# Head attention of a two-stage network: v loaded densely a batch at a time and spread by GpSimd; the TensorE loop moved within its 256-instruction blocks

## What is computed

```python
q, k, v = xs @ Wq.T, xs @ Wk.T, 2 * (xs @ Wv.T)        # 25088 positions, 8 heads x 16
q, k, v_h = _l2norm(q), _l2norm(k), _l2norm(v)
attn_head = softmax(einsum('bnhd,bngd->bnhg', v_h, v_h))      # 8 x 8 a position
q = einsum('bnhg,bngd->bnhd', attn_head, q)
k = einsum('bnhg,bngd->bnhd', attn_head, k)
attn = softmax(einsum('bnhd,bnhe->bnde', k, q))               # 16 x 16 a position
out = einsum('bnhd,bnde->bnhe', v, attn)
out = transpose(out, (0, 3, 1, 2)).reshape(b, n, 128) @ proj_w.T + proj_b
```

## Time and profile before

| what | us |
|---|---|
| three runs | 3550.62, 3564.91 (median), 3569.99 |
| the profiled execution, its own time | 3554.55 |
| its span in the trace | 3552.8 |
| the attention stage in it, about | 1990 to 3424 |
| TensorE's loop in it (33 times) | 2071 to 3313.7 |
| TensorE busy, share of the span | 3015.3 (85%) |
| TensorE weight loads busy | 2232.1 (63%) |
| VectorE busy | 1937.6 (55%) |
| ScalarE busy | 1269.4 (36%) |
| GpSimd busy | 567.8 (16%) |

### The profile page before, as it was taken

One profiled execution on the slowest core, in us unless ns is written; L12 is line 12 of the kernel. 1 busy time (PEld: TensorE's weight loads), 2 busy tenths in 40 slices (PEclk: granted clock), 3 DMA queues, 4 the chain that ended last, 5 costly groups with the idle time before them and its releaser, 6 DMA issues. The chain is left out here.

```text
span 3552.8 us, 145120 instructions
## 1 busy us (share of the span) xinstructions
PE 3015.3 (85%) x62769; PEld 2232.1 (63%) x62769; DVE 1937.6 (55%) x3276; ACT 1269.4 (36%) x2841; POOL 567.8 (16%) x473
## 2 busy tenths in 40 slices
PE   5776989999999999999989677777777777776779
PEld 4553488666666666666644265666666666665679
DVE  4553533666666666666657555455455455454533
ACT  3554443222222222222234344343344343444300
POOL 0000020222222222222211211111111111111100
PEclk7887989999999999999989899888888788888989
DMA  6874000111111111111189444444444444444446
GB/s 151 241 227 127 1 1 1 39 46 44 44 45 45 45 45 44 45 45 45 45 334 397 174 81 74 65 74 66 73 64 76 66 74 66 74 71 70 73 102 206
DMA packets 1033184, 320.17 MB, mean 90 GB/s; under 512 B 872433, under 2 KB 1018414, under 8 KB 1028654
## 3 DMA queue, kind: packets, MB, share of 16 engines
q1 hardware_dynamic: 711058, 182.69, 23.6%
q10 hardware_dynamic: 321692, 130.88, 13.5%
HBM read 157.66 MB, written 155.75 MB: 88 GB/s over the span
## 5 line engine op out<-in xcount | busy, mean ns | idle before, releaser
L845 DVE TENSOR_TENSOR terms<-spec,ps_z 112x456 f32<-112x456 f32 x1024 | 575.5, 624 | 403.2 <-PE ps_z L728 403.1
L738 PEld LDWEIGHTS ps_q<-inv_w,prod 112*57 112x57 f32 x16384 | 450.9, 133 | 174.1 <-issue 172.2
L738 PE MATMUL ps_q<-inv_w,prod 112*57 112x56 f32 x16384 | 484.4, 217 | 0.8 <-DVE prod L851 0.8
L1166 PE MATMUL ps_s<-v_blocks 128*64 128x64 f32 x6272 | 276.6, 257 | 223.5 <-issue 162.1
L728 PE MATMUL ps_z<-x_half,fwd_w 120*112 120x456 f32 x1024 | 458.8, 571 | 0.0
L826 POOL TENSOR_TENSOR prod<-terms 112x456 f32<-112x456 f32 x256 | 297.5, 1162 | 1000.4 <-DVE terms L845 1000.4
L783 ACT ACTIVATE q_half<-ps_q 121x448 f32<-121x448 f32 x255 | 138.8, 544 | 827.3 <-PE ps_y L746 827.3
L1166 PEld LDWEIGHTS ps_s<-v_blocks 128*64 128x64 f32 x6272 | 254.2, 169 | 241.1 <-issue 195.0
L1129 POOL TENSOR_TENSOR k_blocks<-k_mixed,same_of 128x896 f32<-128x896 f32 x112 | 188.1, 1679 | 1185.2 <-ACT k_mixed L1277 1185.2
L1339 DVE TENSOR_TENSOR e_blocks<-s_exp,same_of 128x896 f32<-128x896 f32 x112 | 122.2, 1091 | 364.9 <-ACT s_exp L1262 364.9
L1177 PE MATMUL ps_l<-q_mixed,k_blocks 32*64 32x64 f32 x12544 | 280.3, 247 | 40.1 <-issue 39.1
(11 more groups left out here) (135 smaller groups left out, 4237.5 us busy)
## 6 DMA issues: line engine op xcount, KB each, us to landing
qk_heads<-st_qk ACTq DMA_DIRECT2D x56, 476.0 KB
qk_rows<-qk_heads SPq DMA_DIRECT2D x112, 238.0 KB, 5.0
conv_in<-v_sb ACTq DMA_DIRECT2D x112, 224.0 KB, 3.3
v_in<-conv_in SPq DMA_DIRECT2D x512, 49.0 KB
conv_out<-y_sb ACTq DMA_DIRECT2D x512, 49.0 KB
y<-conv_out SPq DMA_DIRECT2D x8, 1792.0 KB, 12.7
v_blocks<-v_heads SPq DMA_DIRECT2D x896, 14.0 KB, 3.0
x_in<-in_x SPq DMA_DIRECT2D x8, 1568.0 KB, 9.4
```

The source lines that it names most:

```text
L738: last = pe.matmul(ps_q[64 * ri:64 * ri + NF, c * SIDE:(c + 1) * SIDE], prod[b % 2][:, x, c * NF:(c + 1) * NF], k.inv_w[:, x, ri * SIDE:(r ...
L845: last = dve.tensor_tensor(terms[b % 2][:, x, :], k.spec[0:NFFT, s, bass.ds(c * CC, CC), :].rearrange("p c f -> p (c f)"), ps_z[b % 2][z][ ...
L1166: last = pe.matmul(to, vb[m][:, g, a, :], vb[m][:, g, a, :], start=True, stop=True)
```

## The change

It has two parts.

1. `load_v(n)` loads the v of a whole batch (two units) with 8 DMAs into `v_dense`, `[128, 56, 8]`, of which there are four buffers; the rows are dense there, while each piece in DRAM is still the 32 bytes of one position and channel. GpSimd's `spread_v(u)` multiplies the unit's half of it, repeated 8 times, with a mask `slot_of_8` of ones and zeros and writes the whole of `v_blocks` (128 x 1792). `scores` waits for that (`vb_r`), and the wait for the qk load moves to `mix` (`qk_loaded`). The clearing of `v_blocks` goes.
2. 80 instructions that only increment an otherwise unused semaphore stand before TensorE's first projection. With two waits that are new in the unrolled rounds, the loop body begins 82 instructions later in TensorE's list. The body has 1731 instructions then.

```diff
+            def load_v(n):
+                if n >= NB:
+                    return
+                if n >= NV:
+                    sp.wait_ge(vb_r, 2 * (n - NV) + 2)
+                sp.wait_ge(st_stored[n % 2], 32 * (n // 2 + 1))
+                v = t.VT[n * 2 * UT:(n + 1) * 2 * UT].rearrange("(x a q) (d h) -> a q d x h", q=4, a=2, h=HEADS)
+                for a in range(2):
+                    for q in range(4):
+                        sp.dma_start(vd[n % NV][64 * a + q:64 * a + 64:4], v[a, q]).then_inc(v_loaded[n % NV], 16)
...
             for u in range(NU):
-                turn(u)
+                load_qk(u)
                 load_xn(u + AU + 1)
+                if u % 2 == 0:
+                    load_v(u // 2 + 1)
...
+            def spread_v(u):
+                n, g0 = u // 2, u % 2 * 2 * GU
+                if u % 2 == 0:
+                    pool.wait_ge(v_loaded[n % NV], 128 * (n // NV + 1))
+                if u >= RING:
+                    pool.wait_ge(o_ps, u - RING + 1)
+                pool.tensor_tensor(vb[u % RING][:].rearrange("p g r (m h) -> p (g r) m h", h=HEADS),
+                                   bcast(vd[n % NV][:, g0:g0 + 2 * GU], 2, 8),
+                                   bcast(k.slot8[:].rearrange("p (m h) -> p m h", h=HEADS), 1, 2 * GU), ALU.mult).then_inc(vb_r, 1)
...
             for i in range(NU):
                 spread_k(i)
+                if i + 2 < NU:
+                    spread_v(i + 2)
...
-            def scores(i, m, loads):
-                pe.wait_ge(in_loaded[m], loads * 144)
+            def scores(i, m):
+                pe.wait_ge(vb_r, i + 1)
...
-            def mix(i, m):
+            def mix(i, m, loads):
+                pe.wait_ge(qk_loaded[m], loads * 16)
                 pe.wait_ge(e_r, i + 1)
...
+            for _ in range(80):
+                pe.sem_inc(aligned, 1)
```

More of the change, by code:

```diff
@@ L97, in load_weights @@
                      (k.fwd_w[:], t.c_fwd_w), (k.tap_p[:], t.c_tap_p), (k.tap_q[:], t.c_tap_q),
-                     (k.inv_w[:], t.c_inv_w), (k.dc[:], t.c_dc), (k.inv_h[:], t.c_inv_h), (k.same4[:], t.c_same4), (k.same8[:], t.c_same8),
+                     (k.inv_w[:], t.c_inv_w), (k.dc[:], t.c_dc), (k.inv_h[:], t.c_inv_h), (k.same4[:], t.c_same4), (k.same8[:], t.c_same8), (k.slot8[:], t.c_slot8),
                      (k.rpe_in[0:2, :], t.L0_conv_rpe_in_w.rearrange("o i -> i o")),
@@ L1043, in attend @@
     RING = 3
+    NV = 4
     LOOPED = (NU - AU) // RING
@@ L1062, in attend @@
         vb = [sb(f"v_blocks{m}", [128, GU, 2, 64]) for m in range(RING)]
+        vd = [sb(f"v_dense{m}", [128, 4 * GU, HEADS]) for m in range(NV)]
         qk = [sb(f"qk_rows{m}", [128, GU + 1, QKW]) for m in range(RING)]
@@ L1077, in attend @@
         st_stored = [sem(f"st_stored{m}") for m in range(2)]
-        in_loaded = [sem(f"in_loaded{m}") for m in range(RING)]
-        cleared, k_r, qkv_ps, qkv_read = sem("cleared"), sem("k_blocks_ready"), sem("qkv_ps"), sem("qkv_read")
+        v_loaded = [sem(f"v_dense_loaded{m}") for m in range(NV)]
+        qk_loaded = [sem(f"qk_loaded{m}") for m in range(RING)]
+        cleared, vb_r, k_r, qkv_ps, qkv_read = sem("cleared"), sem("v_blocks_ready"), sem("k_blocks_ready"), sem("qkv_ps"), sem("qkv_read")
         nsq_r, nsc_r, nrm_r, rn_r, st_r, vn_r = (sem(n) for n in ("nsq_ready", "nsq_clamped", "nrm_ready", "rnorm_ready", "st_ready", "v_norm_ready"))
@@ L1083, in attend @@
         l_ps, l_exp, z_r, zi_r, p_r = (sem(n) for n in ("l_ps", "l_exp_ready", "z_ready", "z_inv_ready", "p_ready"))
-        o_ps, o_r, mix_seen = sem("o_ps"), sem("o_ready"), sem("mix_seen")
+        o_ps, o_r, mix_seen, aligned = sem("o_ps"), sem("o_ready"), sem("mix_seen"), sem("loop_aligned")
         block = ctx.enter_context(nc.Block())
@@ L1098, in load_xn, with load_qk @@
                 sp.dma_start(xn[w % RING][:], t.XN[b, :, c * UT:(c + 1) * UT]).then_inc(xn_loaded[w % RING], 16)
-            def turn(u):
-                at = slice(u * UT, (u + 1) * UT)
+            def load_v(n):
[8 more added lines that the diff above has]
+                        sp.dma_start(vd[n % NV][64 * a + q:64 * a + 64:4], v[a, q]).then_inc(v_loaded[n % NV], 16)
+            def load_qk(u):
                 m, n = u % RING, u // 2
                 if u < RING:
-                    sp.wait_ge(cleared, m + 1)
+                    sp.wait_ge(cleared, 1)
                 else:
-                    sp.wait_ge(o_ps, u - RING + 1)
+                    sp.wait_ge(o_r, u - RING + 1)
                 sp.wait_ge(st_stored[n % 2], 32 * (n // 2 + 1))
[L1108 to L1115, removed]
+                sp.dma_start(qk[m][:, 0:GU, :], t.QK[u * UT:(u + 1) * UT].rearrange("(g n) h x -> (n h) g x", n=16)).then_inc(qk_loaded[m], 16)
             for w in range(AU + 1):
                 load_xn(w)
+            load_v(0)
             for u in range(NU):
-                turn(u)
+                load_qk(u)
                 load_xn(u + AU + 1)
+                if u % 2 == 0:
+                    load_v(u // 2 + 1)
         @block.gpsimd
@@ L1136, in copy_norm @@
                 pool.tensor_copy(st_qk[a][:, :, :, QKM], nrm[a][:, :, 16:24]).then_inc(vn_r, 1)
+            def spread_v(u):
[7 more added lines that the diff above has]
+                                   bcast(k.slot8[:].rearrange("p (m h) -> p m h", h=HEADS), 1, 2 * GU), ALU.mult).then_inc(vb_r, 1)
             for m in range(RING):
-                pool.memset(qk[m][:, GU:, :], 0.0)
-                pool.memset(vb[m][:], 0.0).then_inc(cleared, 1)
+                last = pool.memset(qk[m][:, GU:, :], 0.0)
+            last.then_inc(cleared, 1)
             for n in range(AHEAD - 1):
                 copy_norm(n)
+            spread_v(0)
+            spread_v(1)
             for i in range(NU):
                 spread_k(i)
+                if i + 2 < NU:
+                    spread_v(i + 2)
                 if i % 2 == 0 and i // 2 + AHEAD - 1 < NB:
@@ L1207, in round_of @@
                 if unit(i):
-                    scores(i, j, c + 1)
+                    scores(i, j)
                 if unit(i - 1):
@@ L1214, in round_of @@
                 if unit(i):
-                    mix(i, j)
+                    mix(i, j, c + 1)
                 if unit(i - 1):
                     outputs(i - 1, (j - 1) % RING)
+            for _ in range(80):
+                pe.sem_inc(aligned, 1)
             for w in range(AU):
@@ L1477, in build @@
         k.dc = sb("zero_freq", [1, NFFT])
-        k.same4, k.same8 = sb("same_of_4", [128, 4]), sb("same_of_8", [128, 64])
+        k.same4, k.same8, k.slot8 = sb("same_of_4", [128, 4]), sb("same_of_8", [128, 64]), sb("slot_of_8", [128, 64])
         k.fwd_h, k.fwd_w = sb("fwd_h", [64 + SIDE, 2 * NF]), sb("fwd_w", [120, 2, NFFT])
@@ L1525, in tables @@
     c["c_same8"] = np.tile(np.kron(np.eye(8), np.ones((HEADS, HEADS))), (2, 1))
+    p = np.arange(128)
+    c["c_slot8"] = np.repeat((4 * (p // 64) + p % 4)[:, None] == np.arange(8), HEADS, axis=1)
     q, p = np.meshgrid(np.arange(NFFT), np.arange(TAPS), indexing="ij")
```

## The result

The changed kernel takes 3361.4 us, the median of four runs (3359.58 to 3362.94), against 3566.1 for the kernel before beside it (3550.62 to 3569.99): a ratio of 0.943, interval 0.9405 to 0.9462. That is 205 us less, where 107 had been forecast. The time lies in the range, but the gain isn't made up as the prediction's sum says.

A forecast was written before the change was run, and what follows sets the result against it. TensorE was taken to wait for code fetched in blocks every pass, load waits close behind. Place -92, loads -30 and -6, start +6, VectorE held by GpSimd +15: -107 from 3554.55, rounded to 3445 us; range 3335 to 3520.

The forecast's parts named there:

- 2 + 1731 = 1733 is 6.8 blocks: 7 are fetched: TensorE's loop, moved by 82 instructions: one block fewer fetched in each pass, 2.8 us a pass, 92 us less.
- the 4.41 us: TensorE's loop before: mean interval between block entries, taken as how long a block takes when fetching is the limit.
- its sentence on crossings: Skill text on instruction fetch: crossing a block is mostly hidden; by that the gain would be the first rival's, 9%.
- No wait of `scores` for a DMA: Sign that the forecast is right: in TensorE's list of waits, `scores` no longer waits for loads.
- The 36 us: Waits of `scores` for loads: a gain of 30 us in the loop and 6 in the rounds after it.
- The lock: VectorE's two-input operations stand still while GpSimd works; `st_v` held by `spread_v` delays the mask for `mix`: +15 us.
- `mix` waits for `e_blocks` in more than a third of the units: Sign that the forecast is wrong through VectorE standing still during GpSimd's work: TensorE's `mix` waits for the mask.
- the two prices (3.36 and 4.57): GpSimd's `spread_v` of 1792 elements: 3.36 us by the `k_blocks` row, which was taken, or 4.57 by `prod`.
- The forecast's own range: Whole kernel: 3385 to 3505 us from the bounds of the forecast's terms, given 68%.
- rival 2: TensorE's instruction fetches speed up as well, to 3.88 us a block: another 105 us, 3340 us; 12%.
- the third: Rival: GpSimd's `spread_v` at 4.57 us delays the mask 3.4 us in 56 units, +190, nothing hidden: 3622 us; 6%.
- Passes shorter than 32 us: Sign that the forecast is wrong: TensorE's loop passes this short would mean that fetches sped up.

The follow-up runs named there:

- the loads alone: The changed kernel without its 80 increments, so the loop touches eight blocks: 3654.7 us, ratio 1.0296 to the kernel before.

## Why the prediction was right and wrong

**What bounds the kernel** was read rightly: code fetched in blocks of 256, in every pass, and load waits close behind. The count of blocks touched held as well: 8 before, 7 after.

**Part 2, the step that failed** is the one behind "2 + 1731 = 1733 is 6.8 blocks: 7 are fetched", in every pass, with a branch that stays, worth -92. None of them is fetched again, and the branch no longer waits for the first, together -300: 183 us less idle time of TensorE, 129 from a higher granted clock, and some 12 of increments against them. The sum had no term for the clock, although the working names the slow matmuls behind a pause. The working took 8.9 fetches a pass as a property of any loop; the trace of before showed only that a loop of eight blocks and one ahead isn't kept, and held no loop of seven. Nor were the 4.41 us the time of a fetch alone: 2.3 to 2.8 us pass from its start to the block's first matmul, and the rest until the next one starts. The mechanism "they stay, from some size on" with the price of all pauses was missing from the rivals. It could have been priced: the branch alone is 4.6 us a pass, 153 us of 33. The 80 increments, counted at nothing or 1.4 us, cost 10.6: taking a block's fetching pace for the pace of a semaphore instruction was wrong by nine times.

The Trainium skill, in "Runtime: NRT & Kernel Launch", section "Instruction fetch mechanics", gives TensorE 128 KiB for instructions. At the 16.4 KB a block of the earlier trace rows that is eight blocks. The runs agree, if one block is counted for what is fetched ahead: seven touched stay, eight don't. The prediction cited its sentence on crossings, which its rows spoke against, and not this one, which decided.

**Part 1, the loads.** "No wait of `scores` for a DMA" came true. The 36 us counted for it were a third of what taking qk out of the wait is worth with v still loaded into its slots: 113.6, because the waits grow to 121.6 us once the fetches are gone. Each part was priced against the old pass, where the other part's limit hid it.

**The lock** was named with its place, its victim, and a hold of `st_v` of 3.4 us (4.47 in the timeline, 4.3 on average), but sized at +15 behind the fetch waits. Before the discount the working had 2.3 us in 56 units, 129 us; 123.2 us in 49 places came. It measured +219.5 with no fetch waits to hide it, and the loads part lost 103 even with them. The reason for discounting was wrong on both counts, and wrong by its own numbers: a block of 4.41 us with 3.7 us of work covers 0.7 us of a lateness of 2.3, not most of it. Nor, by the start times of the fetches with the loads alone, do they go on while TensorE waits for the mask. The sign that the prediction named for it came: `mix` waits for `e_blocks` in more than a third of the units, 49 of about 100. `spread_v` takes 4.1 us, between the two prices (3.36 and 4.57); 0.55 us of the hold shown come after GpSimd's end, and `outputs` runs slower behind nearly every wait of 2.5 us, mostly 2.6 to 3.3 us long.

**The range held the time** by luck: two large terms were both too small, with opposite signs, -300 for -92 and +220 for +15. The forecast's own range, 3385 to 3505, missed 3361.4; it lies in what was added for rival 2. Fetches did not speed up, as rival 2 has it, they stopped. Of the rivals only the third's mechanism shows, and its sign as well, 2.5 us of lateness in each second unit; its 3622 us did not come, because the place was worth 300. "Passes shorter than 32 us" was listed as the sign that fetches had sped up; the 31.1 us had the other cause.

## What to carry to other kernels

When a trace shows instruction fetches in every pass of a TensorE loop, count the blocks of 256 that the loop touches. Here eight to seven was worth all its fetches at once, and 80 instructions ahead of the loop did it, best placed where the engine waits anyway. Count the clock with each pause that goes: 129 of the 312 us that the loop lost were faster matmuls. Don't hand VectorE's partner one long operation: price it by the whole time for which VectorE's two-input operations stand, with their queue, and cut it into pieces before anything else. A wait in front of a fetch isn't hidden by the fetch, unless the trace shows that the fetch goes on meanwhile. Where two limits nearly coincide, price each part of a change with the other limit taken away as well.

## What the runs showed of the hardware

- A loop of 1731 instructions that touches 7 blocks stays with TensorE: a branch of 0.21 us and no fetch between its first and last branch, against a branch of 4.4 to 4.8 us in the median and about 9 fetches a pass with 8 blocks touched. With 11 instructions in the eighth block, 14 of 32 passes fetch.
- Semaphore increments alone follow each other on TensorE at 0.156 us, three times their 51 ns.
- In the pass of the earlier trace rows a block's fetch starts 1.2 to 3.0 us after TensorE has entered the block ahead of it, and its transfer takes about 1 us of the 4.41 from block to block. With a late mask in between, in the run with the loads alone, one started 6.1 us after.
- GpSimd slows down too where it meets VectorE: the copy `st_qk` takes 1.05 us on average in the changed kernel's stretch, where it mostly ends 0.1 us behind VectorE's `e_blocks`, and 0.24 before. 1792 elements take 4.13 us in one instruction and 6.0 in four; a piece of the four takes 1.12 us at its shortest and 2.13 at its longest.
